# A Macaron block with a Mamba-2 mixer on one core: operations of the opening, the chunk steps and the units in another order

## The chip, the cores and the metric

The kernel runs on 1 core of one Trainium2 chip. The metric is the device time of one execution, in microseconds. Engines: PE is TensorE, DVE is VectorE, ACT is ScalarE, POOL is GpSimd, SP is SyncE, which issues most of the DMAs.

## What is computed

The input is x, 2048 tokens of 512 values. With LN a layer norm without weights:

```python
x = x + 0.5 * ffn(LN(x))      # ffn: a 512x512 weight of 4 bits with scales and zeros, plus LoRA, plus bias
x = x + attn(LN(x))
x = x + 0.5 * ffn(LN(x))      # the same ffn

def attn(u):
    h = u + mamba2(rmsnorm(u, ln1_w))        # h is the residual of what follows
    h2 = rmsnorm(h, ln2_w)
    return h + silu(h2 @ gate_w.T) * (h2 @ up_w.T) @ down_w.T      # 1792 wide

def mamba2(x):                               # 4 heads of 128, state 128, chunks of 128 tokens
    z, xBC, dt = split(x @ w_in.T)           # 512, 768 and 4 columns
    xBC = silu(causal_conv(xBC, 4 taps) + conv_b)
    ...                                      # per chunk: decay, (C B^T * decay) X, and the carried state
    return ((Y + D * xs) * silu(z)) @ w_out.T
```

## The kernel before

Everything is one program in which the order of each engine's instructions is written out by hand, with semaphores between the engines. An engine takes its instructions strictly in that order, so whatever waits holds up all that is written behind it. Products are made in f16 with each operand split into a high part (ACT rounds) and a low part (DVE subtracts, the functions `lo...`), three products for one (`PARTS`).

The 2048 tokens are 16 chunks of 128 (`c`), four to a tile of 512 (`i`, and `j` the place in the tile). The work has four stages.

**Opening** (to about 42 us; its end on DVE is L1749 to L1780, on ACT L1017 to L1051, on PE L2191 to L2219). The FFN weight is made from its 4 bits. The first six chunks are normed (`prep0`, `hi0`), transposed on PE (`first_t0`), copied (`tc0`), put through the FFN in f32 (`first_f`), added (`x1_stats`, which also makes the statistics for the next norm) and normed again (`hi1`, `lo1`). POOL makes each norm's factors from the statistics, in the order `ln1_chain(3)`, `ln0(5)`. Beside this, two scales are found, powers of two: one for the FFN weight, one for `w_in`. For each, a maximum per partition goes through a transpose on PE (`max_turn`), a reduction on DVE (`max_row`), a spread on PE (`max_spread`) and a chain of small DVE instructions (`max_all`, `power_of_two`). ACT waits for both (L1049) before it makes the high part of `w_in`.

**Prologue** (to about 87 us). `w_in` is cut, tile 0 is projected (`proj`), convolved (`taps`, three DVE instructions over 512 columns each), and put through silu. Chunks 6 to 9 come in. On SP's queue the transfers that transpose a chunk stand in order: `t1(6)` (second norm's input of chunk 6, after `lo1(6, 2)`), `next_x(6)`, `t0(8)` (first norm's output of chunk 8, after `lo0(8, 0)`), `t1(7)`, and so on. PE's `f(8)`, at the start of step 0, needs `t0(8)`. ACT's `hi1(7)` needs `t1(6)`.

**Steps** (`step(c)`, to about 345 us), one per chunk. PE does the FFN of chunk c + 8, the scan of chunk c, its output product `w(c)`, and some projections of the next tile; in the last four chunks gate/up products stand in their place. Three PSUM banks go round among these products, and a planner at L298 to L322 notes for each what must have freed its bank: for `f(11)` and `f(15)` it is `residual2` of chunk 2 and of chunk 6, and for the projection of plane 8 of tile 3 it is that of chunk 10. `residual2` (L1444) adds the product of `w(c)` to the norm and frees its bank; where `j` is 2, it stands behind the taps of plane 5 (`slot_a`). The scan of chunk c + 1 is prepared in step c: ACT's `scan_decay`, DVE's `scan1` (makes S), POOL's `scan_d` (masks S and adds the diagonal, L555), which PE's `s2_diag` (L2053) needs. Ahead of these stand, for chunk c - 1, the high part (`hi2`, ACT, needs POOL's factor `r2`) and the low part (`lo2`, DVE, L1379) of the norm whose transposed form gate/up reads. The gate on y (`gate_y`, L1428) frees PE for `w(c)`. From chunk 10 on POOL also makes sums of tokens for the last stage (`sums`).

**Units** (`unit(m)`, to about 702 us). Gate/up for the other six pairs of the 1792 columns run as seven products in place of eight (Strassen), four units to a pair, with the down products between them. In the last unit of a pair (`n == 3`), ACT (`st_a(p + 1, 0)`, L1074 and L1077) and DVE (`st_g(p + 1)`, L1533) make the two parts of the next pair's gate weight, with which PE's next unit starts. ACT's `evict` takes a down product out of PSUM, and POOL adds it to x by DMA. Then the last FFN runs over the chunks.

Of the kernel before, what the change touches and what calls it, by code (L numbers as in the profile page):

```python
# [6 lines left out]
ALU = mybir.AluOpType  # L7
# [7 lines left out]
P = 128  # L15
EPS = 1e-5
ACT_SCALE = 2.0 ** 9
# [10 lines left out]
def build(nc, x_in, w_in_t, conv_w, conv_b, a_log, d_skip, dt_bias, w_out_t, ln1_w, ln2_w,  # L28
# [23 lines left out]
    with ctx:  # L52
# [704 lines left out]
        def _(ac):  # L757
# [170 lines left out]
            def step(c):  # L928
                i, j = divmod(c, CH)
                a = c + 2 * CH  # L930
                if c > 0:
                    i_late, late = (c - 1) // CH + 1, SLOTS[(c - 1) % CH][1:]
                if c + 1 < NCH:
                    scan_ecs(c + 1, (c + 1) % CH)
                    scan1(c + 1, (c + 1) % CH)
                if c > 0 and i_late < NS:
                    for q in late[1:]:
                        slot_a(i_late, q)
                    slot_b(i_late, late[0])
                if a + 1 < NCH:  # L940
                    hi0(a + 1, (a + 1) % CH)
                if c > 0 and i_late < NS:
                    for q in late[1:]:
                        slot_b(i_late, q)
                if c > 0:
                    hi2(c - 1, (c - 1) % CH)
                if c + 1 < NCH:
                    scan_decay(c + 1, (c + 1) % CH)
                if j == 2 and i + 1 < NS:
                    slot_a(i + 1, SLOTS[j][0])  # L950
                if a < NCH:
                    hi1(a, a % CH)
                if c + 1 < NCH:
                    scan2(c + 1, (c + 1) % CH)
                if c == 3 * CH:
                    t_his(0, 0, 1, 2, 3)
                renorm(c)
                if c == 3 * CH + 2:
                    t_his(1, 0, 1, 2, 3)
                if i + 1 < NS:  # L960
                    if j != 2:
                        slot_a(i + 1, SLOTS[j][0])
                    slot_b(i + 1, SLOTS[j][0])
                    if j == 0:
                        sp_exp(i + 1)
                else:
                    gate_a(0, j)
                    gate_b(0, j)
                square(c, j)
                if i + 1 < NS:  # L970
                    slot_a(i + 1, SLOTS[j][1])
                if c in (2 * CH - 2, 2 * CH - 1):
                    fold(c - (2 * CH - 2))
                if c == 2 * CH + 2:
                    cut_a()
                if c == 2 * CH + 3:
                    cut_b()
# [60 lines left out]
            tc0(3)  # L1038
            hi1(0, 0)
            w_in_sum(2)  # L1040
            hi1(1, 1)
            hi0(4, 0)
            w_in_sum(3)
            tc0(4)
            hi1(2, 2)
            hi1(3, 3)
            hi0(5, 1)
            tc0(5)
            ac.wait_ge(e_scale, 2)  # L1049
            w_in_hi(W_IN_PIECES[0])  # L1050
            w_in_hi(W_IN_PIECES[1])  # L1051

# [140 lines left out]
            def weight_work(p, n, part):  # L1193
                if n == 0 and p > 1:
                    st_b(p, part)
                elif p + 1 < NP:
                    if n == 2:
                        norm(p + 1, part)
                    if n == 3:
                        st_a(p + 1, part)  # L1200

            def unit(m):
# [4 lines left out]
                copy_p1(m)  # L1207
                if m > 0:
                    hi_s(m - 1, 1)
                evict(ds[0])  # L1210
                tanh_s(m, 0)
                if m == 1:
# [42 lines left out]
        def _(ve):  # L1255
# [59 lines left out]
                ve.wait_ge(e_maxT, n + 1)  # L1315
                ve.tensor_reduce(mx1[:, n:n + 1], PS[0:1, B_MAX, MAX_AT[n]:MAX_AT[n] + P], AX_X, ALU.max).then_inc(e_max1, 1)

            def max_all(n):
                ve.wait_ge(e_all, n + 1)
                chain(ve.tensor_copy(mxa[:, n:n + 1], PS[:, B_MAX, MAX_AT[n] + P:MAX_AT[n] + P + 1]))  # L1320

            def ffn_scale():
                max_all(0)
                power_of_two(pw[:, 0:1], sw[:, 0:1], mxa[:, 0:1], chain)
                ve.sem_inc(e_scale, 1)
                chain(ve.tensor_scalar(d_f[:, :], pw[:, 0:1], 0.5 * 2.0 ** -W_TOP / ACT_SCALE, None, ALU.mult))

            def ffn_lo():
                for k in range(KB):
                    ve.wait_ge(e_fhi, k + 1)  # L1330
# [6 lines left out]
                chain(ve.tensor_tensor(mxk[:, :], mxk[:, :], ln1[:, :], ALU.mult))  # L1337
                ve.tensor_reduce(mx[:, 1:2], mxk[:, :], AX_X, ALU.max, apply_absolute_value=True).then_inc(e_max, 1)

            def w_in_scale():  # L1340
                max_all(1)
                power_of_two(pw[:, 1:2], sw[:, 1:2], mxa[:, 1:2], chain)
                chain(ve.tensor_scalar(lsw[:, :], ln1[:, :], sw[:, 1:2], None, ALU.mult))
                ve.sem_inc(e_scale, 1)

            def small_scales():
                chain(ve.tensor_scalar(d_i[:, :], pw[:, 1:2], 2.0 ** -W_TOP / ACT_SCALE, None, ALU.mult))
                chain(ve.tensor_scalar(d_ih[:, :], d_i[:, :], 0.5, None, ALU.mult))
                ve.wait_ge(s_small, 16 * 4)
# [274 lines left out]
            def prologue():  # L1624
# [18 lines left out]
                silu(0, 2)  # L1643
                taps(0, 4)
                silu(0, 3)
                prep0(8, 0)
                taps(0, 5)
                x1_stats(7, 3, PLAN["f", 7][0])
# [3 lines left out]
                silu(0, 5)  # L1652
                silu_z(0, 1)
                prep0(9, 1)
                lo1(6, 2)
                weights(0, 0)
                silu_z(0, 2)
                scan1(0, 0)
# [3 lines left out]
            def step(c):  # L1662
# [29 lines left out]
                    gate_y(c, j)  # L1692
                if c == 2 * CH + 2:
                    scale_read(0)
                if c > 0:
                    lo2(c - 1)
                advance(c, j)
                if c + 1 < NCH:
                    weights(c + 1, (c + 1) % CH)
                    scan1(c + 1, (c + 1) % CH)  # L1700
                if c == 3 * CH:
                    t_los(0, 0, 1, 2, 3)
                if c == 3 * CH + 2:
# [20 lines left out]
                    maximum_gu(1).then_inc(e_max, 1)  # L1724
                if c == 2 * CH + 3:
                    cut_a()
                if i + 1 < NS:
                    slot_a(i + 1, SLOTS[j][0], {1: 9}.get(j))
                    if j == 0:
                        softplus(i + 1, 0)  # L1730
                        softplus(i + 1, 1)
                        softplus(i + 1, 2)
                else:
                    gate_up(0, j)
                residual2(c, j)
                if c == 3 * CH:
                    cut_b()
                if i + 1 < NS:
# [24 lines left out]
            lo1(0, 0)  # L1763
            prep0(4, 0)
            x1_stats(2, 2, B_P[0])
            lo1(1, 1)
            ffn_scale()
            w_in_bound()
            max_row(1)
            x1_stats(3, 3, B_P[1])  # L1770
            prep0(5, 1)
            w_in_scale()
            lo1(2, 2)
            lo1(3, 3)
            w_in_lo(0)
# [56 lines left out]
            def unit(m):  # L1832
# [10 lines left out]
                    lo_s(m - 1, 1)  # L1843
                ve.wait_ge(e_gu, 2 * NS + base + 3)
                ve.tensor_tensor(u2, p1s, p_bank(m, IP6), ALU.add).then_inc(e_add, 1)
                if p + 1 < NP and n == 2 and m > 2:
                    scale_read(p + 1)
                    scales(p + 1)
                    descale(p + 1)
# [10 lines left out]
                if p + 1 < NP:  # L1860
                    if n == 1:
                        bound_g(p + 1, 0)
                        bound_g(p + 1, 1)
                        bounds(p + 1)
                    if n == 3:
                        st_g(p + 1)
                if m == NU - 1:
                    tail(1)
                ve.wait_ge(e_gu, 2 * NS + base + 5)
# [83 lines left out]
        def _(pe):  # L1953
# [254 lines left out]
            first_f(2)  # L2208
            max_spread(0)
            first_f(3)  # L2210
            first_t0(4)
            max_turn(1)
            max_spread(1)
            first_f(4)
            first_t0(5)
# [195 lines left out]
```

## Time and profile before

| | us |
|---|---|
| median of 3 runs | 783.96 |
| lowest, highest | 780.64, 784.36 |
| the profiled execution | 782.24 |
| its span, first to last instruction | 780.5 |
| busy: PE, DVE, ACT, POOL | 756.2, 628.9, 447.0, 336.4 |
| mean granted TensorE clock, share of full | 0.998 |

Busy time is that of the engine's instructions; waiting is not in it. A wait for several semaphores is put down to the one that came last by the profile.

### The profile page before, as it was taken

The numbers are of one execution on the slowest core, as the hardware profiler recorded it, in microseconds if no ns is written. First come the engines' busy times: TensorE is split into PE (matmuls) and PEld (weight loads), VectorE is DVE, ScalarE is ACT, GpSimd is POOL, SyncE is SP. The second block draws the span as 40 slices with busy tenths as digits, with TensorE's granted clock in tenths as the row PEclk, the third lists the DMA queues.
The fourth block names the chain that finished last, engine by engine and source line by source line (L and its number), as shares of the span: only waits on it lengthen the run. The fifth ranks groups of instructions, "written<-read, shape, count | busy, mean of one in ns | idle before, by whom it ended". The sixth has DMA issues, their size and how long they took to land.

```text
span 780.5 us, 10661 instructions
## 1 busy us (share of the span) xinstructions
PE 756.2 (97%) x3470; PEld 352.7 (45%) x3470; DVE 628.9 (81%) x1235; ACT 447.0 (57%) x881; POOL 336.4 (43%) x392
## 2 busy tenths in 40 slices
PE   8899899999999989899999999999999999999998
PEld 3344454454445444444443444444444444444443
DVE  7798678978967888777799979779779779667994
ACT  4777667767675766645435655555555455444441
POOL 5631344563543269664604224224234233224573
PEclk9999999999999999999999999999999999999999
DMA  8832543542431111520241544643643743443565
GB/s 299 188 74 54 130 101 81 109 107 46 83 64 28 38 31 28 135 41 15 43 119 28 136 89 73 149 81 68 157 78 64 162 82 57 81 79 72 119 161 135
DMA packets 95415, 71.86 MB, mean 92 GB/s; under 512 B 65233, under 2 KB 72401, under 8 KB 95361
## 3 DMA queue, kind: packets, MB, share of 16 engines
q0 software_dynamic: 17280, 31.46, 22.6%
q1 hardware_dynamic: 77600, 39.66, 19.7%
q8 instruction: 28, 0.46, 0.3%
q14 instruction: 27, 0.21, 0.1%
q10 hardware_dynamic: 480, 0.07, 0.1%
HBM read 20.32 MB, written 4.19 MB: 31 GB/s over the span
## 4 chain that ended last, share of the span: by engine, by line
PE 65%; DVE 19%; ACT 5%; issue 4%; POOL 4%; DMA 2%; SPq 0%; ACTq 0%; DVEq 0%; POOLq 0%
PE PS L1957 57%; PE PS L2080 3%; DVE raw L1453 2%; DVE st L1284 1%; DVE stage L1453 1%; PE PS L2088 1%; DVE state L1435 1%; DMA x_t<-hb 1%; DVE xs L1385 1%; PE PS L2062 1%; DVE S L1418 1%; PE PS L2053 1%; POOL r L521 1%; ACT pre L884 1%; PE PS L2070 1%
## 5 line engine op out<-in xcount | busy, mean ns | idle before, releaser
L712 POOL DMA_DIRECT2D xs<-x x59 | 50.9, 863 | 150.9 <-ACT x L1157 136.9
L1957 PE MATMUL PS<-h,w_in 128*128 128x512 f16 x480 | 108.7, 379 | 0.1
L1957 PE MATMUL PS<-h,x_t 128*128 128x512 f16 x408 | 94.0, 379 | 0.2 <-DVE pre L1795 0.2
L1957 PEld LDWEIGHTS PS<-h,w_in 128*128 128x128 f16 x480 | 46.8, 98 | 65.3 <-issue 15.4
L1957 PE MATMUL PS<-n_T,stage 128*128 128x512 f16 x288 | 71.5, 379 | 0.0
L1157 ACT ACTIVATE x<-PS,d_d 128x512 f32<-128x512 f32 x59 | 40.2, 682 | 39.4 <-PE PS L1957 39.4
L1957 PEld LDWEIGHTS PS<-h,x_t 128*128 128x128 f16 x408 | 39.5, 98 | 48.9 <-issue 2.7
L521 POOL TENSOR_TENSOR r<-mv,mhalf 128x1 f32<-128x1 f32 (+1 forms) x32 | 28.7, 897 | 75.9 <-DVE mv L1288 62.2
L712 POOL DMA_DIRECT2D xs<-n x29 | 25.2, 869 | 71.8 <-ACT n L1157 61.5
L1957 PE MATMUL PS<-pre,stage 128*128 128x512 f16 x192 | 49.3, 379 | 0.0
L1127 ACT ACTIVATE xds<-tm,dgh 128x512 f32<-128x512 f32 x24 | 17.3, 722 | 50.7 <-DVE tm L1886 50.7
L1957 PE MATMUL PS<-w_ffn,raw_gu 128*128 128x512 f16 x192 | 43.3, 379 | 1.2 <-DMA raw_gu<-raw_d 1.2
L1957 PEld LDWEIGHTS PS<-n_T,stage 128*128 128x128 f16 x288 | 28.1, 98 | 34.0 <-ACT x L1157 0.3
L1453 DVE SCALAR_TENSOR_TENSOR raw<-pre,cw,raw 128x512 f32<-128x512 f32 x36 | 28.0, 777 | 11.1 <-ACT raw L885 10.8
L1957 PE MATMUL PS<-w_ffn,n_T 128*128 128x512 f16 x120 | 29.2, 396 | 6.2 <-DVE x L1444 3.2
L1957 PE MATMUL PS<-raw,x_t 128*128 128x512 f16 x144 | 34.7, 379 | 0.4 <-DVE Ld L1841 0.4
L1957 PE MATMUL PS<-w_in,x_t 128*128 128x512 f16 x144 | 34.8, 379 | 0.0
L1957 PE MATMUL PS<-h,n 128*128 128x512 f16 x144 | 33.2, 379 | 1.5 <-DVE n L1533 1.5
L1157 ACT ACTIVATE n<-PS,d_d 128x512 f32<-128x512 f32 x29 | 19.8, 683 | 23.8 <-PE PS L1957 23.1
L2080 PE MATMUL PS<-w_out,raw 128*128 128x512 f32 x64 | 29.1, 597 | 1.0 <-DVE raw L1428 0.9
L1957 PEld LDWEIGHTS PS<-w_ffn,raw_gu 128*128 128x128 f16 x192 | 18.6, 98 | 24.1 <-DMA raw_gu<-raw_d 1.7
L2080 PE MATMUL PS<-w_out,stage 128*128 128x512 f32 x64 | 29.1, 598 | 0.1
(314 smaller groups left out, 1809.7 us busy)
## 6 DMA issues: line engine op xcount, KB each, us to landing
xs<-x POOLq DMA_DIRECT2D x75, 256.0 KB, 3.3
xs<-n POOLq DMA_DIRECT2D x29, 256.0 KB, 3.3
x_t<-x_in SPq DMA_DIRECT2D x16, 256.0 KB, 3.0
x_t<-hb POOLq DMA_DIRECT2D x16, 256.0 KB, 3.8
out<-x_t SPq DMA_DIRECT2D x16, 256.0 KB, 2.3
raw_gu<-gate_t SPq DMA_DIRECT2D x7, 512.0 KB, 4.5
raw_gu<-up_t SPq DMA_DIRECT2D x7, 512.0 KB, 6.5
raw_d<-down_t SPq DMA_DIRECT2D x7, 512.0 KB, 7.4
```

The source lines that it names most:

```text
L521: return po.tensor_tensor(dst, src, mhalf[:, 0:src.shape[-1]], ALU.pow)
L712: po.dma_start(chunk_of(xs, c), d_tmps[d % 3], accum_op=ALU.add).then_inc(s_acc[d % 3], 16)
L884: ac.activation(pre[:, w, NTAP - 1:], src, ACT.Copy)
L1127: ac.activation(th_s[ab], u4 if ab else c11, ACT.Tanh, scale=dgh[:, p % 2:p % 2 + 1]).then_inc(e_tanh_g, 1)
L1157: ac.activation(d_tmps[d % 3], bank(d_bank(d)), ACT.Copy, scale=d_d[:, p % 3:p % 3 + 1]).then_inc(e_ev, 1)
L1284: link(ve.bn_stats(stat, src), e_link, base + 1)
L1385: link(ve.scalar_tensor_tensor(chunk_of(xs, c), bank(b), 0.5 / ACT_SCALE if c < NF else d_f[:, :], x_t[:, j, :], ALU.mult, ALU.add), e_x1, ...
L1418: last = ve.scalar_tensor_tensor(S[:, s, h, :], heads(B_G)[:, h, :], dt[:, (c // CH) % 2, j * H + h:j * H + h + 1], Ld[:, h, :], ALU.mult, ...
L1435: last = ve.scalar_tensor_tensor(state[:, h, :], state[:, h, :], ecs[:, s, h, P - 1:P], heads(B_SS)[:, h, :], ALU.mult, ALU.add)
L1453: ins = ve.scalar_tensor_tensor(xbc[i % 2][:, b, :], pre[:, w, k:k + ST], cw[:, b, k:k + 1], xbc[i % 2][:, b, :], ALU.mult, ALU.add)
L1957: ins = pe.matmul(out_, lhs(a, b, k), rhs(a, b, k), start=first and n == 0, stop=last and n == len(todo) - 1)
L2080: last = pe.matmul(bank(b), y[:, h, (c % CH) * P:(c % CH + 1) * P], w_out[:, h, :], start=h == 0, stop=h == H - 1)
```

## The change

It touches four places. In the opening, the two scales are found in one chain of instructions (`both_scales`), the sum of the fourth block of `w_in` and the bound move forward, and some norms change places; ACT's wait is for one event instead of two, and `d_f` is made in `small_scales`. In the prologue, `lo1(6, 2)` stands before `prep0(8, 0)`. In the steps, `residual2` stands before `slot_a` where `j == 2` and there is a next tile (chunks 2, 6, 10), and for chunks above 12 `hi2` and `lo2` stand behind `scan_decay` and `scan1`. In the last unit of each pair, the two parts of the gate weight are made earlier.

```diff
@@ scalar, step(c)
-                if c > 0:
+                if 0 < c <= 3 * CH:
                     hi2(c - 1, (c - 1) % CH)
                 if c + 1 < NCH:
                     scan_decay(c + 1, (c + 1) % CH)
+                if c > 3 * CH:
+                    hi2(c - 1, (c - 1) % CH)
@@ scalar, opening
             w_in_sum(2)
+            w_in_sum(3)
             hi1(1, 1)
             hi0(4, 0)
-            w_in_sum(3)
             tc0(4)
             hi1(2, 2)
+            hi0(5, 1)
             hi1(3, 3)
-            hi0(5, 1)
             tc0(5)
-            ac.wait_ge(e_scale, 2)
+            ac.wait_ge(e_scale, 1)
@@ scalar, weight_work
-                    if n == 3:
+                    if n == 3 and part > 0:
                         st_a(p + 1, part)
@@ scalar, unit(m)
                     hi_s(m - 1, 1)
+                if p + 1 < NP and n == 3:
+                    st_a(p + 1, 0)
                 evict(ds[0])
                 tanh_s(m, 0)
@@ vector
-            def max_all(n):
-                ve.wait_ge(e_all, n + 1)
-                chain(ve.tensor_copy(mxa[:, n:n + 1], PS[:, B_MAX, MAX_AT[n] + P:MAX_AT[n] + P + 1]))
-
-            def ffn_scale():
-                max_all(0)
-                power_of_two(pw[:, 0:1], sw[:, 0:1], mxa[:, 0:1], chain)
-                ve.sem_inc(e_scale, 1)
-                chain(ve.tensor_scalar(d_f[:, :], pw[:, 0:1], 0.5 * 2.0 ** -W_TOP / ACT_SCALE, None, ALU.mult))
...
-            def w_in_scale():
-                max_all(1)
-                power_of_two(pw[:, 1:2], sw[:, 1:2], mxa[:, 1:2], chain)
+            def both_scales():
+                ve.wait_ge(e_all, 2)
+                chain(ve.tensor_copy(mxa[:, :], PS[:, B_MAX, :].rearrange("p (n q) -> p n q", q=MAX_AT[1])[:, :, P]))
+                power_of_two(pw[:, :], sw[:, :], mxa[:, :], chain)
                 chain(ve.tensor_scalar(lsw[:, :], ln1[:, :], sw[:, 1:2], None, ALU.mult))
                 ve.sem_inc(e_scale, 1)
 
             def small_scales():
+                chain(ve.tensor_scalar(d_f[:, :], pw[:, 0:1], 0.5 * 2.0 ** -W_TOP / ACT_SCALE, None, ALU.mult))
@@ vector, prologue
                 silu(0, 3)
+                lo1(6, 2)
                 prep0(8, 0)
...
                 prep0(9, 1)
-                lo1(6, 2)
                 weights(0, 0)
@@ vector, step(c)
-                if c > 0:
+                if 0 < c <= 3 * CH:
                     lo2(c - 1)
                 advance(c, j)
                 if c + 1 < NCH:
                     weights(c + 1, (c + 1) % CH)
                     scan1(c + 1, (c + 1) % CH)
+                if c > 3 * CH:
+                    lo2(c - 1)
...
+                if j == 2 and i + 1 < NS:
+                    residual2(c, j)
                 if i + 1 < NS:
                     slot_a(i + 1, SLOTS[j][0], {1: 9}.get(j))
...
-                residual2(c, j)
+                if j != 2 or i + 1 == NS:
+                    residual2(c, j)
@@ vector, opening
             x1_stats(2, 2, B_P[0])
+            w_in_bound()
             lo1(1, 1)
-            ffn_scale()
-            w_in_bound()
+            prep0(5, 1)
             max_row(1)
             x1_stats(3, 3, B_P[1])
-            prep0(5, 1)
-            w_in_scale()
+            both_scales()
@@ vector, unit(m)
                 ve.tensor_tensor(u2, p1s, p_bank(m, IP6), ALU.add).then_inc(e_add, 1)
+                if p + 1 < NP and n == 3:
+                    st_g(p + 1)
...
-                    if n == 3:
-                        st_g(p + 1)
@@ tensor, opening
             first_f(3)
+            max_turn(1)
             first_t0(4)
-            max_turn(1)
             max_spread(1)
```

## Rows read from the trace of the kernel before

**Rows 1.** The page's part 1: busy time and its share of the span.

```profile
PE 756.2 (97%) x3470; PEld 352.7 (45%) x3470; DVE 628.9 (81%) x1235; ACT 447.0 (57%) x881; POOL 336.4 (43%) x392
```

**Rows 2.** Who PE waited for, whole span: total us, times, longest.

```profile
PE PS L1957 <- DVE x L1444: 3.2, 2, 1.7
PE PS L2053 <- POOL S L555: 3.1, 3, 1.2
PE PS L1957 <- DMA n_T<-n_p: 3.0, 2, 2.7
...
PE PS L1957 <- DVE n L1533: 1.5, 1, 1.5
...
PE PS L2080 <- DVE raw L1428: 0.9, 1, 0.9
...
PE PS L1957 <- DVE pre L1795: 0.2, 1, 0.2
```

**Rows 3.** Timeline of the opening, DVE then PE: start, us, instruction, idle before.

```profile
29.03 0.15 DVE L1320 COPY mxa<-PS 128x1 f32<-128x1 f32 x1
...
31.19 0.67 DVE L1385 SCALAR_TENSOR_TENSOR xs<-PS,x_t 128x512 f32<-128x512 f32 x1
...
32.97 0.68 DVE L1284 BATCH_NORM_STATS2 st<-x_t 128x6 f32<-128x512 f32 x1
...
42.11 5.34 PE L1957 MATMUL PS<-h,w_in 128*128 128x512 f16 x24
```

**Rows 4.** Timeline of the prologue's end; the last row is busy time by window.

```profile
83.44 0.68 DVE L1367 TENSOR_TENSOR hn_p<-hn,hn_p 128x512 f16<-128x512 f32 x1
...
84.32 2.75 PE L1957 MATMUL PS<-h,w_in 128*128 128x512 f16 x12
...
86.10 2.26 SPq L443 DMA_TRANSPOSE n_T<-n_p  x1
...
87.37 1.26 POOL L555 TENSOR_TENSOR S<-S,d_diag 128x512 f32<-128x512 f32 x1
...
90.24 4.45 PE L1957 MATMUL PS<-w_ffn,n_T 128*128 128x512 f16 x12 [2.71 <-DMA n_T<-n_p]
...
91.00:92.00 1.00, 1.00 (x4) 0.30 (x2) 0.07 (x1) 1.00 (x4) 0.00 (x0) 0.50 0.00 0
```

**Rows 5.** Timeline of steps 2 and 3, then of step 7: DVE and PE.

```profile
143.38 2.31 DVE L1453 SCALAR_TENSOR_TENSOR raw<-pre,cw,raw 128x512 f32<-128x512 f32 x3
145.60 0.68 DVE L1444 TENSOR_TENSOR x<-n,PS 128x512 f32<-128x512 f32 x1
...
152.15 0.74 DVE L1428 SCALAR_TENSOR_TENSOR stage<-PS,d_ih,stage 128x512 f32<-128x512 f32 x1
...
155.08 3.60 PE L2080 MATMUL PS<-w_out,stage 128*128 128x512 f32 x8
...
222.45 0.74 DVE L1428 SCALAR_TENSOR_TENSOR raw<-PS,d_ih,raw 128x512 f32<-128x512 f32 x1
...
224.50 3.60 PE L2080 MATMUL PS<-w_out,raw 128*128 128x512 f32 x8
```

**Rows 6.** Timeline of PE in steps 10 to 12.

```profile
280.94 1.12 PE L2045 MATMUL PS<-raw 128*128 128x512 f32 x2 [0.45 <-DVE raw L1461]
...
291.98 1.12 PE L2053 MATMUL PS<-S,tm 128*128 128x512 f32 x2 [0.85 <-POOL S L555]
```

**Rows 7.** Timeline of step 13, ACT and DVE.

```profile
311.56 0.72 ACT L794 ACTIVATE h2n_p<-x,r 128x512 f16<-128x512 f32 x1 [2.70 <-POOL r L521]
...
312.31 1.95 DVE L1379 SCALAR_TENSOR_TENSOR h2n_p<-x,r,h2n_p 128x512 f16<-128x512 f32 x1
```

**Rows 8.** All of one line, L1379: shortest, median, longest in ns.

```profile
L1379 DVE SCALAR_TENSOR_TENSOR h2n_p<-x,r,h2n_p x16: 740/754/1945, 119.7 to 348.2; 128x512 f16<-128x512 f32 x16
```

**Rows 9.** Timeline of unit 3, ACT then DVE.

```profile
424.11 0.61 ACT L1074 ACTIVATE n<-raw_gu 128x512 f16<-128x512 f32 x1
...
425.72 0.68 DVE L1533 TENSOR_TENSOR n<-raw_gu,n 128x512 f16<-128x512 f32 x1
```

## The prediction

> **What bounds the kernel now.** I read the page first. TensorE (PE) is busy 756.2 of 780.5 us [rows 1], so only 24 us of the span is not matrix work, and an edit that moves work on another engine pays only where it takes away one of PE's waits. The next view is therefore who PE waited for [rows 2]. The first five pairs shown come to 11.7 us. Then I read the timeline round each wait: what the releasing instruction stood behind, and what comes next if it is released sooner. The profiled execution took 782.2 us, 1.7 outside the span. The median of the runs is 784.0 with one run at 780.6, so a measurement can tell about 0.5% (4 us) from no change.
>
> **Opening scales: 0.5 us.** In the old order VectorE (DVE) makes the FFN scale in a chain of small instructions from 29.03, bounds w_in, waits for the transposed maximum, and only at 31.19 starts `x1_stats(3)` [rows 3]: 2.2 us for little work. Now the FFN copy and its four steps go, `d_f` moves into `small_scales` (its cover is w_in's low part, which PE needs only two projections later), and in their place stands `prep0(5,1)`, 1.0 us (from 32.97, 0.68 and two small ones) [rows 3]. `w_in_sum(3)` goes ahead of `hi1(1,1)` on ScalarE (ACT), so `lo1(1,1)` starts perhaps 0.4 later. I get `x1_stats(3)` at 29.03 + 0.4 + 1.0 + 0.2 for `max_row` = 30.65, 0.5 sooner. GpSimd (POOL) makes chunk 3's and then chunk 5's norm factors behind it, so `hi0(5,1)` can start near 34.6; but now `hi1(3,3)` (two activations, 1.4) stands behind it and before `tc0(5)`. The last transpose copy, hence `first_f(5)` and the projection that started at 42.11 [rows 3], gain the same 0.5. Also for PE, `max_turn(1)` ahead of `first_t0(4)` saves nothing more: the transpose waits for ACT there anyway. What is late next is `t1(3)`: `lo1(3,3)` is about 1 us later, and its transfer must land before 41.6. Bounds: 1.5 gained at best (`both_scales` comes 1.0 + 0.5 sooner on DVE), 1.4 lost at worst (the pair now ahead of `tc0(5)`). I take 0.5, since POOL's factors limit both.
>
> **The seventh chunk's split: 4.4 us, the largest term.** `lo1(6,2)` ran at 83.44 though its input was ready at about 73. SP's queue is in order: `t1(6)` waits for it, and `next_x(6)` and `t0(8)` stand behind. So chunk 8's transpose was issued at 86.10, and PE stood 2.71 us before `f(8)` [rows 4]. Worse, the granted clock is 0.50 from 91 to 92, that is 1.2 GHz instead of 2.4: it fell behind this idle time, and the 12 matmuls of `f(8)` took 4.45 us where the 12 at 84.32 took 2.75 [rows 4]. Moved ahead of `prep0(8,0)`, the split is done by 75, and `t0(8)` waits for `lo0(8,0)` alone, which by the timeline ended near 80.5 and is 0.6 later as the moved instruction is now ahead of it. It is issued at 81.1, and even 4.1 us later (86.10 to 90.24) it is there by 85.3, before PE is ready at 87.5. Gain: 2.71 + (4.45 - 2.75) = 4.4. Next comes `s2_diag(0)`, which needs POOL's sum at 87.37 + 1.26 [rows 4]; 0.6 later that is 89.2, and PE gets there at 90.1. That cover is 0.9 us; if it goes, the term loses what is missing. `hi1(7,3)` no longer waits for `t1(6)` either, so chunk 7's transpose, due at the next projection, goes forward with it. Bounds: 2.7 (only the wait goes) and 4.4.
> The page "TensorE: Matmul & The Clock Gate" of the Trainium skill (Part 1) says that the array goes back to half clock when it has been idle, and comes up again only with work. By it the two halves stand or fall together: if any wait of this size stayed, the 1.7 us would stay too. The trace agrees so far, as it shows both here and neither where the wait was 1.7.
>
> **Residual ahead of the taps: +1.6, +0.7, -0.6.** In chunks 2 and 6, `f(11)` and `f(15)` use the bank that `residual2` empties, and it stood behind three conv taps: 143.38 to 145.60, 0.68 long itself [rows 5]. PE waited 3.2 us in the two [rows 2]. First in line it frees the bank 2.2 sooner, so both waits go. The price is 0.6 on the taps, the tanh, the silu and all of DVE's next step, up to `gate_y`. After chunk 2 `gate_y` ended at 152.89 for an output product at 155.08; PE comes 1.7 earlier and y 0.6 later, so 1.6 of 1.7 is kept. After chunk 6 it ended at 223.19 for 224.50: 1.3 of slack less 0.6 leaves 0.7 of 1.5 [rows 5]. In chunk 10 PE did not wait for the residual; it waited 0.45 for the silu at 280.94 [rows 6], and that is now 0.6 later, as is ACT's square, from which POOL's chain leads to the wait of 0.85 at 291.98 [rows 6]. Both give 0.6 lost, once. Bounds for all three: +3.2 (the waits) and -1.8 (0.6 each time).
>
> **Last block's second norm: 3.3 us.** In the step of chunk 13 ACT stood 2.70 us for POOL's factor before `hi2(12)`, with the decay of chunk 14 behind it; on DVE `lo2(12)` took 1.95, with the state and `scan1(14)` behind it [rows 7]. S then went to POOL, and PE waited for POOL's sum. Decay and scan don't need the norm. With them first, ACT can start the decay near 308.8, DVE does `scan1(14)` about 1.9 sooner (the whole `lo2`), and the sum is ready near 316.6 where PE wants it at 317.3. The same holds a step on. The three waits for this sum came to 3.1, of which 0.85 is the one above that stays: 2.2 goes. The 0.9 for y in the last step [rows 2] goes as well, since tanh, gates and tile sums all come sooner: 3.1, and the wait for the gated product (0.2) [rows 2] too: 3.3. The norm itself is later by the decay and scan, some 1.5 us; its cover is that only the transposes for gate/up read it, steps away. Bounds: 0 and 3.3.
> `lo2` takes 0.75 in the median, yet 1.95 here [rows 7, 8], with POOL busy beside it. The Trainium skill's page "SBUF — State Buffer" says ("SBUF: two separate sides") that a VectorE operation with two SBUF inputs and a GpSimd operation exclude each other for a whole instruction. This speaks against the move: `lo2` now starts as POOL begins on S. By it POOL's sum would come one `lo2` later, 317.3, level with PE's need, and the term would be 3.2 rather than 3.3.
>
> **Units: 1.1 us.** PE waited 1.5 for the low part of the next gate weights, done at 426.4 [rows 2, 9]. ACT's high part moves ahead of an eviction and a tanh, and DVE can make the low part, at 425.72 before, ahead of one product and one addition of 0.6 each [rows 9]: 1.2 sooner, and 0.1 goes to the next weights, which DVE finishes no sooner. In the four later pairs PE did not wait, so nothing there; the eviction is 0.9 us later (the pair from 424.11), covered by PE's next product, and so is POOL's transfer behind it. Bounds: 0 and 1.5.
>
> **Sum.** 0.5 + 4.4 + 1.6 + 0.7 - 0.6 + 3.3 + 1.1 = 11.0 us. Against the profiled run: 782.2 - 11.0 = 771.2; against the median 773.0. I say 772, between them.
>
> **Rivals.**
> - *The steps keep nothing.* DVE is on much of the chain through the steps, and a wait taken from PE comes back one link later: tap delay three times, the POOL sum held up by `lo2`. Then only opening, split and units count: 784.0 - 6.0 = 778.0. For: DVE and ACT wait for one another there. Against: the slack read off above. Chance 0.2.
> - *The split's wait stays.* `t0(8)` lands no sooner than f(8) needs it, or the POOL sum behind it takes the place and the clock falls all the same: 784.0 - 6.6 = 777.4. Against: 2 us of room. Chance 0.1.
> - *Nothing comes of it*, because the queue order that I read is not what holds the waits, within 4 us of 784: chance 0.09.
> - *Slower.* `t1(3)` lands late: its split is behind `hi1(3,3)`, itself behind `hi0(5,1)`, and the first projection stands long enough for the clock to fall. A matmul at half clock costs (4.45 - 2.75)/12 = 0.14 us more. To lose the 11.0 and 4 more, some 105 matmuls must run so, more than the 72 that come before the first conv product, with the idle time on top; time 789. Against: `f(8)` shows the clock back within 12. Chance 0.03.
> - The forecast: 0.58.
>
> **Range and chances.** The forecast's own terms give 768 (every wait goes, no delay counted, the faster base) to 776; the first two rivals end near 778, and I stop at 779. Faster by over 0.5%: 0.58 + 0.2 + 0.1 = 0.88; within: 0.09; slower: 0.03.
>
> **What would show it.** PE's waits should lack the DMA wait before `f(8)`, both waits for `residual2`, and two of three for POOL's sum; the granted clock should stay at 1.00 past 80 us; `f(8)` should take 2.75. The projection should start near 41.6. The silu wait near 270 (280.94 less what is gained) should be 1.0, not 0.45. I am wrong if PE's idle time falls by less than 6 us, or if a new wait of over 1 us stands at the output product of chunk 3 or 7, or at `s2_diag`.

## The result and the profile after

The changed kernel takes 774.97 us (median of 5 runs, 774.16 to 776.01), the kernel before 783.19 in the same series: ratio 0.9899, 95% interval 0.9877 to 0.992, faster by 1.0%. The forecast was 772.0 with a range of 768 to 779. The sign and the largest term held; some 3 us of the expected 11 are missing. The profiled execution took 775.83 us, 1.7 outside its span of 774.1, against 782.24 and 780.5. Two of the five executions of the changed kernel, this one and the one at 776.01, had a mean granted clock of 0.998; the other three, 774.16 to 774.97, had 1.000. Of the executions further down two took far longer, one of the kernel with the residual of chunk 10 moved back (988.02 us) and one of the kernel before (1614.6): they count in the medians and not in the ratios.

Part 1 of the page of the changed kernel, against [rows 1]:

```profile
PE 755.7 (98%) x3470; PEld 352.5 (46%) x3470; DVE 628.5 (81%) x1230; ACT 446.0 (58%) x881; POOL 337.5 (44%) x392
```

The work of PE is the same to 0.5 us, so the change could act through waits and the clock alone. PE's idle time fell from 24.33 to 18.35 us, by 5.98: the prediction had named less than 6 as a sign of being wrong, and this is just under it. Who PE waited for in the changed kernel (total us, times, longest), against [rows 2]:

```profile
PE PS L1957 <- ACT n L1159: 1.6, 3, 0.6
...
PE PS L1957 <- ACT x L1159: 1.2, 2, 0.6
...
PE PS L2045 <- DVE raw L1457: 1.0, 1, 1.0
PE PS L2080 <- DVE raw L1424: 0.9, 1, 0.9
PE PS L2053 <- POOL S L555: 0.8, 1, 0.8
...
PE PS L1957 <- DVE n L1529: 0.3, 1, 0.3
PE PS L1957 <- DMA n_T<-n_p: 0.2, 1, 0.2
PE PS L2080 <- DVE stage L1424: 0.2, 1, 0.2
```

All that was to go has gone: the residual's 3.2, two of the three waits for POOL's sum, the transpose's 2.7, 1.2 of the gate weights' 1.5. But two rows are new: five waits, 2.8 us together, for the eviction (now L1159) in the units. No new wait of over 1 us stands at the places that the prediction had named (0.86 at the output product of chunk 7, 0.83 at `s2_diag`). The timeline of PE in the changed kernel, at the places that the forecast named:

```profile
37.48 5.40 PE L2180 MATMUL PS<-h,n_T 128*128 128x512 f32 x8 [1.23 <-ACT n_T L774]
...
88.39 2.75 PE L1957 MATMUL PS<-w_ffn,n_T 128*128 128x512 f16 x12
90.98 1.02 PE L2053 MATMUL PS<-S,tm 128*128 128x512 f32 x2
...
150.00 1.55 PE L2080 MATMUL PS<-w_out,stage 128*128 128x512 f32 x3 [0.18 <-DVE stage L1424]
...
218.86 1.13 PE L2080 MATMUL PS<-w_out,raw 128*128 128x512 f32 x2 [0.86 <-DVE raw L1424]
...
276.00 1.12 PE L2045 MATMUL PS<-raw 128*128 128x512 f32 x2 [1.05 <-DVE raw L1457]
...
416.31 2.76 PE L1957 MATMUL PS<-h,n 128*128 128x512 f16 x12 [0.33 <-DVE n L1529]
424.80 0.82 PE L1957 MATMUL PS<-pre,w_out 128*128 128x512 f16 x3 [0.43 <-ACT n L1159]
...
468.93 0.82 PE L1957 MATMUL PS<-pre,w_out 128*128 128x512 f16 x3 [0.57 <-ACT n L1159]
```

To see where the 6.4 us of the two spans lie, I cut both executions at the first projection and at seven one-matmul landmarks, the transposes of the maxima (PE, L2121). The first, second, third, fourth and seventh of them in the changed kernel:

```profile
255.07 0.27 PE L2121 MATMUL PS<-ident,mx 128*3 128x128 f32 x1 [0.52 <-ACT raw L885]
335.78 0.27 PE L2121 MATMUL PS<-ident,mx 128*3 128x128 f32 x1
392.70 0.27 PE L2121 MATMUL PS<-ident,mx 128*3 128x128 f32 x1 [0.55 <-DVE mx L1481]
444.32 0.27 PE L2121 MATMUL PS<-ident,mx 128*3 128x128 f32 x1
...
619.15 0.27 PE L2121 MATMUL PS<-ident,mx 128*3 128x128 f32 x1
```

and in the kernel before:

```profile
260.61 0.27 PE L2121 MATMUL PS<-ident,mx 128*3 128x128 f32 x1 [0.52 <-ACT raw L885]
344.72 0.27 PE L2121 MATMUL PS<-ident,mx 128*3 128x128 f32 x1
401.64 0.27 PE L2121 MATMUL PS<-ident,mx 128*3 128x128 f32 x1 [0.55 <-DVE mx L1485]
453.66 0.27 PE L2121 MATMUL PS<-ident,mx 128*3 128x128 f32 x1
```

(its seventh is at 626.18). With the projection at 42.11 before and 43.14 after, the stretches are:

| stretch | before | after | difference |
|---|---|---|---|
| to the first projection (opening) | 42.11 | 43.14 | +1.03 |
| to the 1st transpose (split, residual of chunks 2 and 6) | 218.50 | 211.93 | -6.57 |
| to the 2nd (last block: residual of chunk 10, second norm) | 84.11 | 80.71 | -3.40 |
| to the 3rd | 56.92 | 56.92 | 0 |
| to the 4th (units, first pair end) | 52.02 | 51.62 | -0.40 |
| to the 7th (units, three pair ends) | 172.52 | 174.83 | +2.31 |
| to the end (one more pair end) | 154.32 | 154.95 | +0.63 |

The losses are at both ends: 1.0 us in the opening, 2.9 in the units.

### The profile page after: what moved, and what is told of

The parts are those of the page before. It is cut to its first block, busy times and chain, and to the rows that moved or that the text cites. A ratio compares the mean times of both kernels' runs of the same rounds, so it can differ in the third digit from the quotient of the medians.

```text
span 774.1 us, 10655 instructions
## 1 busy us (share of the span) xinstructions
PE 755.7 (98%) x3470; PEld 352.5 (46%) x3470; DVE 628.5 (81%) x1230; ACT 446.0 (58%) x881; POOL 337.5 (44%) x392
## 4 chain that ended last, share of the span: by engine, by line
PE 67%; DVE 20%; ACT 5%; issue 4%; DMA 2%; POOL 2%; ACTq 0%; POOLq 0%; DVEq 0%
PE PS L1957 55%; PE PS L2080 4%; DVE raw L1449 2%; DVE S L1817 2%; DVE xds L1819 1%; PE PS L2088 1%; DVE st L1288 1%; PE PS L2180 1%; DVE stage L1449 1%; PE PS L2053 1%; DMA x_t<-hb 1%; PE PS L2062 1%; DVE state L1431 1%; PE PS L2070 1%; PE PS L2045 1%
## 5 line engine op out<-in xcount | busy, mean ns | idle before, releaser
L1159 ACT ACTIVATE x<-PS,d_d 128x512 f32<-128x512 f32 x59 | 40.2, 682 | 41.2 <-PE PS L1957 41.2
L1159 ACT ACTIVATE n<-PS,d_d 128x512 f32<-128x512 f32 x29 | 19.8, 684 | 24.8 <-PE PS L1957 24.8
L1957 PEld LDWEIGHTS PS<-pre,stage 128*128 128x128 f16 x192 | 18.7, 98 | 23.5 <-ACT x L1159 1.1
```

What stands on the lines that cost most here:

```text
L1159: ac.activation(d_tmps[d % 3], bank(d_bank(d)), ACT.Copy, scale=d_d[:, p % 3:p % 3 + 1]).then_inc(e_ev, 1)
L1957: ins = pe.matmul(out_, lhs(a, b, k), rhs(a, b, k), start=first and n == 0, stop=last and n == len(todo) - 1)
```

## The experiments

The landmarks resolve 0.1 us where a median of four runs does not resolve 1, so the sizes below are read from the stretches, the verdicts on kernels from the medians. Each kernel is the changed one with one edit, unless said. "Before" stood at a median of 782.57, 783.29 and 783.12 us in the three series, and the ratios are to it. Where an experiment is set beside the changed kernel, the two medians are from different series.

**The split back in its old place, and the split alone.**

```
                 silu(0, 3)
-                lo1(6, 2)
 ...
                 prep0(9, 1)
+                lo1(6, 2)
```

> The changed kernel with the seventh chunk's split back in its old place, all else changed. Theory: it is the largest term and stands alone: 4.4 us in the forecast, 4.57 between the two profiles; the wait of 2.7 us for the chunk's transpose before the FFN product at 90 us returns, with the clock at half for the product's 4.45 us. From the projection to the second product at 91 us it takes 4.4 to 4.6 us more than in the changed kernel. Rival (part of it was given by the residual's or the opening's new place, or is given back later): under 3 us on the median.

Measured: 778.68 us (ratio 0.9947, 0.9929 to 0.9965), 3.7 above the changed kernel. The stretch to the first transpose is 258.13 - 41.55 = 216.58, against 211.93 in the changed kernel and 212.1 in most of the other kernels here that have both edits: 4.5 us. The timeline of PE with the split in its old place, and its windows (us busy by engine, then the granted clock):

```profile
89.75 4.45 PE L1957 MATMUL PS<-w_ffn,n_T 128*128 128x512 f16 x12 [2.63 <-DMA n_T<-n_p]
```

```profile
91.00:92.00 1.00, 1.00 (x4) 0.31 (x3) 0.40 (x1) 1.00 (x3) 0.00 (x0) 0.50 0.23 54
```

Both halves return, the wait of 2.63 and the product at half clock, as in [rows 4].

The other way round, the kernel before with this one edit:

> The kernel before with the seventh chunk's split in its new place and nothing else. Theory: the split's term is independent of the other edits: no wait for the chunk's transpose at 90 us, and from the first projection to the first transpose of maxima 4.4 us less than the 218.50 of the kernel before, 214.1; median 4 us under that of before, a little less than 4.4 since some runs of the kernel before show a clock of 1.000 and can win only the wait of 2.7. Rival (the split needs the residual's or the opening's new places to be of use): 216 or more, and a median within 2.5 us of before.

Measured: 779.24 us (0.995, 0.993 to 0.997), 3.9 under before; 257.51 - 43.54 = 213.97 us to the first transpose, 4.5 less. The term does not depend on the rest. By difference (218.50 - 216.58) the residual's move in chunks 2 and 6 is worth 1.9, where the forecast had 2.3; the two places in the timeline gave 1.5 and 0.6.

**The opening as it was.** Both scale chains, the order on ACT and PE and the places of `w_in_sum(3)`, `prep0(5, 1)` and `hi0(5, 1)` as before.

```
-            hi0(5, 1)
             hi1(3, 3)
+            hi0(5, 1)
             tc0(5)
-            ac.wait_ge(e_scale, 1)
+            ac.wait_ge(e_scale, 2)
 ...
-            both_scales()
+            w_in_scale()
```

> The changed kernel with its opening as before (both scale chains, the old order of ACT and PE). Theory: the opening's new order costs 1.03 us up to the first projection (it starts at 43.14 instead of 42.11), because two idle stretches close together (0.79 and 1.23 us) let the clock fall and the first FFN product of chunk 5 took 5.40 us instead of 3.70. Then this kernel's projection starts at 42.1 and its span is about 1.0 us shorter than the changed kernel's 774.1, the granted clock between 20 and 40 us level with before. Rival (the 1.0 us is lost in the transfers, w_in's low part or the split behind the opening, or what is lost at the start is covered later): span within 0.4 us of 774.1.

Measured: 776.55 us (0.992, 0.9894 to 0.9947), span 775.6: 1.5 us longer than the changed kernel's, where 1.0 shorter was expected. The theory fell. Timeline of PE with the old opening:

```profile
37.09 0.66 PE L2179 MATMUL PS<-ident,n 128*128 128x128 f32 x4 [1.21 <-ACT n L767]
38.44 5.40 PE L2189 MATMUL PS<-h,n_T 128*128 128x512 f32 x8 [0.69 <-ACT n_T L774]
...
44.10 2.11 PE L1966 MATMUL PS<-h,w_in 128*128 128x512 f16 x9
```

The two waits are the 1.2 and 0.7 of the kernel before, whose product took 3.70; here it took 5.40. So the old opening loses the clock too, in some executions. And the new one keeps it in most. The next rows are PE's in the kernel with the units' edit in the first pair alone (below), whose opening is the changed kernel's, with the same two waits:

```profile
35.71 0.66 PE L2172 MATMUL PS<-ident,n 128*128 128x128 f32 x4 [0.80 <-ACT n L767]
37.60 3.70 PE L2182 MATMUL PS<-h,n_T 128*128 128x512 f32 x8 [1.23 <-ACT n_T L774]
...
41.57 4.70 PE L1959 MATMUL PS<-h,w_in 128*128 128x512 f16 x21
```

Windows of the changed kernel, then of that one, 36 to 41 us: PE is busy 3.77 us in both, the granted clock (third figure from the end) 0.70 and 1.00.

```profile
36.00:41.00 5.00, 3.77 (x8) 1.61 (x7) 2.70 (x6) 5.00 (x11) 3.31 (x5) 0.70 0.77 151
```

```profile
36.00:41.00 5.00, 3.77 (x12) 1.66 (x11) 2.58 (x6) 5.00 (x11) 3.44 (x5) 1.00 0.80 158
```

Of nine profiles with the new opening, the changed kernel's alone shows the fall; of three with the old, two (this one and the kernel with the split alone). Like with like, the projection starts at 42.11 (old) against a median of 41.6 (new, eight profiles, 41.28 to 43.16) where the clock held, and at 43.5 and 44.1 against 43.14 where it fell. That has the sign and about the size of the forecast's 0.5 us, but the scatter of the opening from run to run (1.9 us among the eight) is larger, so the size is not shown.

**The transpose copy ahead of chunk 3's pair.**

```
             hi0(5, 1)
-            hi1(3, 3)
             tc0(5)
+            hi1(3, 3)
```

> The changed kernel with the transpose copy of chunk 5 right behind its normalization, ahead of the pair of activations for the transpose of chunk 3. Theory: PE's second idle stretch (1.23 us before the FFN product of chunk 5) shrinks to 0.5 us or less, the clock does not fall, the product takes 3.7 us or less and starts at about 36.8; the projection then starts between 41.0 and 41.6, 1.5 to 2 us sooner than in the changed kernel, span 772.1 to 772.6. Rival 1 (the clock falls with the first of the two stretches all the same): the product starts at 36.8 but takes 5.4, projection at 42.4. Rival 2 (the transpose of chunk 3 comes late for the projection, since its split is now later): a wait for a transfer of up to 1 us at the first projection.

Measured: 775.13 us (0.9908, 0.9883 to 0.9934); the projection starts at 42.35. PE's timeline:

```profile
37.03 3.70 PE L2180 MATMUL PS<-h,n_T 128*128 128x512 f32 x8 [0.69 <-ACT n_T L774]
40.79 0.38 PE L2163 MATMUL PS<-junk 128*128 128x512 bf16 x1
42.35 1.46 PE L1957 MATMUL PS<-h,w_in 128*128 128x512 f16 x6 [1.19 <-DMA h<-hn_p]
```

The second rival held: the FFN product is early (37.03) and at full clock, and the projection waits 1.19 us for chunk 3's transpose, issued at 39.27 by SP's queue and used 3.1 us later. In the changed kernel it is issued at 37.76, so it is there at about 40.9, 0.7 ahead of an undisturbed projection. The order of the change has little left in either direction.

**Idle matmuls where PE waits.** They compute nothing that is used.

```
             first_f(4)
+            keep_warm(3)
             first_t0(5)
+            keep_warm(4)
```

> The changed kernel with seven idle matmuls into a free bank: three before the transpose of chunk 5's input, four behind it, where PE waited 0.79 and 1.23 us. They do no work for the result. Theory: what the opening loses is the clock, not the waits, so with PE kept busy the FFN product of chunk 5 takes 2.9 to 3.7 us instead of 5.40 and the projection starts 1.2 to 1.7 us sooner, near 41.7, though nothing else is earlier. Rival (the product took long for another reason, such as the wait for its operand or weight loads): the product still takes over 5 us and the projection starts at 43.1 or later, as seven matmuls were added.

Measured: 774.94 us (0.9905, 0.988 to 0.993); the product takes 3.70, the projection starts at 42.05. The number came out as forecast, but it shows less than I meant it to: the product takes 3.70 without ballast as well in most profiles, and then the projection starts at 41.6, sooner than with it. That the 5.40 came from the clock is read from the granted clock of 0.70 above, not from this experiment.

**The residual of chunk 10 back behind the taps.**

```
-                if j == 2 and i + 1 < NS:
+                if j == 2 and i < 2:
                     residual2(c, j)
 ...
-                if j != 2 or i + 1 == NS:
+                if j != 2 or i >= 2:
                     residual2(c, j)
```

> The changed kernel with the residual of chunk 10 back behind the conv taps, those of chunks 2 and 6 still ahead of them. Theory: PE did not wait for that residual, so its early place only delays the taps and the silu; the wait for the silu at 276 us falls from 1.05 to 0.45 and the stretch between the first two transposes of maxima is 0.6 us shorter than 80.71, span and median 0.6 lower. Rival (the delay is absorbed, as POOL's sum is what PE waits for next, and that comes at the same time): less than 0.2 us.

Measured: 773.8 us (0.9873, 0.9836 to 0.991), 1.2 below the changed kernel; the stretch is 333.57 - 253.42 = 80.15, against 80.71: 0.56. The forecast's -0.6 was right, and nothing absorbs it in this stage. The wait for the silu is back to 0.4. (The other 0.6 us of the 1.2 is not explained by the edit; medians of series differ by that much.)

**The last block's second norm: both halves back, one at a time.** On ACT (with `hi2`) and on DVE (with `lo2`):

```
-                if 0 < c <= 3 * CH:
+                if c > 0:
                     lo2(c - 1)
 ...
-                if c > 3 * CH:
-                    lo2(c - 1)
```

> The changed kernel with the second norm of the last block ahead of the decay again, on ACT and on DVE. Theory: the stretch from the first to the second transpose of maxima (255.07 to 335.78 in the changed kernel, 80.71 us; 84.11 before) is back at 84.1 plus the 0.6 of the residual of chunk 10, so 84.1 to 84.7: the term is 3.4 to 4.0 us, against 3.3 in the forecast. PE's waits for POOL's sum return to 3 us. Rival (the DVE and POOL operations that now run beside one another slow each other, so that part comes from elsewhere): under 2.5 us.

Measured: 778.47 us (0.9939, 0.992 to 0.9958), 3.5 above; the stretch is 338.94 - 254.23 = 84.71, so the term is 4.0. PE's waits in the whole of that kernel:

```profile
PE PS L2049 <- POOL S L555: 3.0, 3, 1.2
PE PS L2076 <- DVE raw L1422: 1.7, 2, 0.9
```

The three waits for POOL's sum are back, and beside the 0.86 of chunk 7 that the residual's move left, the 0.88 of the last y.

Only DVE's half back:

> The changed kernel with the low part of the last block's second norm ahead of the decay on DVE again, its high part still behind it on ACT. Theory: DVE then waits for a high part that ACT makes only behind the decay, so both halves are lost and a little more: the stretch between the first two transposes of maxima is 84.7 to 85.7 us, against 80.7 with both halves and 84.7 with none. Rival (it is ACT's half that counts and DVE's small instruction is covered): under 83.

Measured: 339.92 - 255.21 = 84.71 (one run, 779.83 us). Only ACT's half back:

> The changed kernel with the high part of the last block's second norm ahead of the decay on ACT again, its low part behind it on DVE. Theory: ACT stands for POOL's factor with the decay behind it (2.7 us), but DVE no longer puts its 1.9 us in between, so about half of the term stays: 82 to 83.3 us between the first two transposes of maxima. Rival (DVE's half does nothing without ACT's): 84.7.

Measured: 336.45 - 253.71 = 82.74 (one run, 776.36 us). So moving ACT's half alone is worth nothing (the low part then stands on DVE, waiting for it, with the scan behind), moving DVE's alone 2.0, both 4.0. Each rests on one execution.

**The eviction in the units.** First, the early high and low part in the first pair alone:

```
-                if p + 1 < NP and n == 3:
+                if m == 3:
                     st_a(p + 1, 0)
                 evict(ds[0])
```

(`st_g` on DVE likewise, and both in their old places for later pairs.)

> The changed kernel with the early high and low part of the next gate weights only in the first pair of units; in the five later pair ends the order is as before. Theory: the two activations (0.83 us) ahead of the eviction make PE wait 0.43 to 0.60 us for the evicted bank, at each pair end, and cost about 0.77 each with what follows; in the first pair the gain of 1.2 outweighs it. So the four later ones give back 3.1 us: span 771.0, and PE's waits for the eviction fall from 2.8 us to about 0.4. Rival (the landmarks drift in the units because of something else, such as the DVE order or the clock): the drift stays, span 774.

Measured: 771.59 us (0.9863, 0.9834 to 0.9892), span 769.6. From the first to the seventh landmark it takes 615.46 - 253.71 = 361.75, against 364.08: 2.3 less, and 0.8 less behind it (154.14 against 154.95). Second, in all pairs, but the eviction first:

```
+                evict(ds[0])
                 if p + 1 < NP and n == 3:
                     st_a(p + 1, 0)
-                evict(ds[0])
```

> The changed kernel with the eviction ahead of the two activations of the next gate weights in every pair of units, both still ahead of the tanh. It tells whether PE's loss in the units comes from the eviction's place (the two activations stand before it) or from the tanh's and the gate weights'. Theory: the eviction alone. Then the wait for the evicted bank goes in all five pairs, also in the first, and from the first transpose of maxima (255 us in the changed kernel) to the last (619) it takes 3.5 us less than the changed kernel's 364.1, about 360.6, or 0.4 less than the experiment with the first pair alone (361.8 there). Rival (the tanh behind the activations is what comes late, or the early low part on DVE): 364, as the eviction's place does not matter.

Measured: 771.28 us (0.9842, 0.9811 to 0.9873), 361.72 from first to seventh. ACT and PE at the second pair end, in the changed kernel:

```profile
467.38 0.61 ACT L1076 ACTIVATE n<-raw_gu 128x512 f16<-128x512 f32 x1
467.90 0.40 ACT L1079 ACTIVATE d_diag<-raw_gu 128x256 f16<-128x256 f32 x1
468.21 0.67 ACT L1159 ACTIVATE n<-PS,d_d 128x512 f32<-128x512 f32 x1
```

with PE at 468.93 [0.57], and with the eviction first:

```profile
465.64 0.67 ACT L1159 ACTIVATE n<-PS,d_d 128x512 f32<-128x512 f32 x1
466.21 0.62 ACT L1076 ACTIVATE n<-raw_gu 128x512 f16<-128x512 f32 x1
466.73 0.40 ACT L1079 ACTIVATE d_diag<-raw_gu 128x256 f16<-128x256 f32 x1
467.04 0.71 ACT L1129 ACTIVATE xds<-Ld,dgh 128x512 f32<-128x512 f32 x1
```

The tanh is as late as in the changed kernel, counted from the first of these instructions (1.4 us in both), the low part as early, and the loss is gone: the eviction's place alone made it. The 360.6 was missed by 1.1: in the first pair the order makes no difference. There PE's wait of 0.43 for an eviction at the next unit (424.80) stays in both, since ACT comes to it straight from the high parts, which wait for DVE.

**The two corrections together** (eviction first, residual of chunk 10 behind the taps):

> The changed kernel with the eviction ahead of the activations of the next gate weights, and with the residual of chunk 10 behind the conv taps. Theory: the two corrections lie in different stages and add up: 771.28 less 0.6 is 770.7 us, the stretch between the first two transposes of maxima 80.15 and that from the second to the last 280.97, span 768.7. Rival (in the last block the gain of the residual is eaten by the wait for maxima or for the low part of the gate weights): 771.3.

Measured: 771.35 us (0.9859, 0.984 to 0.9878), not distinguishable from the 771.28 with the eviction alone. The stretches are 80.15 and 281.25: half of the residual's 0.6 is given back in the units (281.25 against 280.97). Both kernels beat the changed one, by 3.6 and 3.7 us; the second correction adds nothing that the medians show.

## Why the prediction came out as it did

- **Split, 4.4: right.** 4.5 by undoing it and 4.5 by doing it alone. What was said of the clock held: wait and half clock left together and came back together. It is not a fixed price: of the 16 runs of before in one series, two had a mean granted clock of 1.000 and took 780.9 and 781.0, against a median of 783.3, so there presumably only the wait is to be won (their traces were not taken).
- **POOL's sum next, cover 0.9: mis-sized, without effect.** It was ready at 90.66 for a PE at 90.98: 0.3 was left.
- **Residual, +1.6 and +0.7: right**, 1.5 and 0.6 in the timeline, 1.9 by the stretch. The wait for y came to 0.18 and 0.86, as the slack read off in [rows 5] said. **-0.6: right**, 0.56.
- **Last block's second norm, 3.3: right in mechanism, too small.** The four waits that it named (1.21 and 1.00 for POOL's sum, 0.23, 0.88) came to 3.3 and all went; the term measured 4.0. The other 0.7 is what a wait costs beside its own row. The product behind one is longer, 1.12 or 1.13 for 1.02 at `s2_diag`, 3.70 for 3.60 at the output product: 0.31. And a row counts from the end of PE's row before, while an undisturbed product starts 0.16 before that end (at 304.62, when the row before, 0.39 from 304.39, ends at 304.78): 0.64 for the four. Against it 0.28 is left in the changed kernel at 312.37, where no wait is shown but the product starts 0.17 later than an undisturbed one and takes 1.13. 3.32 + 0.31 + 0.64 - 0.28 = 3.99, for a measured 4.0. The cover of 0.7 that it computed was used up: the sum ended at 312.32 for a PE that took it at 312.37. Of what used it up, 0.45 is POOL's L553, which stands ahead of the sum and took 1.09 us beside `lo2` at 309.88, against 0.64 at 316.48 in the kernel before. The prediction's other reading, "level with PE's need", is what came.
- **Units, 1.1: the step that failed.** "In the four later pairs PE did not wait, so nothing there; the eviction is 0.9 us later (the pair from 424.11), covered by PE's next product". The first half is true and says nothing, since a row without a wait does not tell how much slack it has. The cover was some 0.1 us. In the kernel before, the eviction of the second pair end ended at 477.35 for the product that needs its bank at 477.50, and 0.05 lies between the two where PE waits (468.88 and 468.93):

```profile
476.68 0.67 ACT L1157 ACTIVATE n<-PS,d_d 128x512 f32<-128x512 f32 x1
...
477.50 0.81 PE L1957 MATMUL PS<-pre,w_out 128*128 128x512 f16 x3
```

Counted from the landmark before it, the eviction starts 0.87 later in the changed kernel (23.89 against 23.02) and the product 0.77 (24.61 against 23.84), of which PE's row shows 0.57. The row is short for the reason given above. A period between landmarks grows by the same 0.77, from 57.51 to 58.28. Four of them lose 3.1. In the first pair the gate product did start 1.2 sooner, but 0.8 of it was lost again by the fourth landmark, 0.43 as the wait at 424.80. Together -2.5 instead of +1.1.
- **Opening, 0.5: not contradicted, its size not shown.** In the profiled execution a clock that fell there by chance hides it (+1.03 in the ledger: 1.7 lost to the clock, 0.7 gained before it). The link that was computed is there, `x1_stats(3)` starts at 30.67 for a forecast of 30.65. What reaches the projection lies within the scatter of 1.9.

For the medians that makes 0.5 (the forecast's own, as no run gives a better figure) + 4.5 + 1.9 - 0.6 + 4.0 - 2.5 = 7.8 us, and 8.2 were measured. None of the rivals came. The range held because it reached down to partial gains, not because this loss had been seen.

## What to carry to other kernels

An instruction moved ahead of another on an in-order queue taxes every iteration, also those in which nothing was late. Before a cover is claimed, measure it: the time from the delayed instruction's end to the start of what waits for it (0.15 us here, against a delay of 0.87), not the absence of a wait. Put the early work behind the one that frees a PSUM bank: it costs the early work 0.6 us here and saves 0.77 in each later pair. And where two halves of a value sit on two engines, moving one half alone may bring nothing (here 0 and 2.0 against 4.0 for both).

## What was not expected of the hardware

- **The same two short waits do and don't cost the clock.** With 0.7 to 0.8 and then 1.23 us of waiting (new order) PE's granted clock over 36 to 41 us was 0.70 in one profile and 1.00 in eight; with 1.2 and 0.7 (old) it fell in two of three. A fall costs 1.7 us, 5.40 for the product instead of 3.70. The Trainium skill's page "TensorE: Matmul & The Clock Gate" (Part 1) says that the point of the transition varies from run to run, as it doesn't hang on where the kernel starts. It says so of the rise at the start of work; in these profiles the same holds of a fall behind short waits in mid-kernel. One pair of profiles can therefore not price such an opening, and my first theory was built on one.
- **DVE's `lo2` and POOL's instructions take turns.** In the last block's new order `lo2` took 2.52 us at 319.50 where the median is 0.75, and of POOL's instructions beside it the sum took 1.61 where the median is 1.27:

```profile
319.50 2.52 DVE L1375 SCALAR_TENSOR_TENSOR h2n_p<-x,r,h2n_p 128x512 f16<-128x512 f32 x1 [0.65 <-ACT h2n_p L794]
```

```profile
319.36 1.52 POOL L549 TENSOR_TENSOR raw<-raw,ecs 128x512 f32<-128x512 f32 x1
320.58 0.89 POOL L553 TENSOR_SCALAR_AFFINE_SELECT S<-S 128x512 f32<-128x512 f32 x1
321.55 1.61 POOL L555 TENSOR_TENSOR S<-S,d_diag 128x512 f32<-128x512 f32 x1
```

It cost nothing, since S was there at 323.16 for a PE at 324.55. POOL's L549 had begun 0.14 before `lo2`, and `lo2` ended at 322.02, 0.55 after the end of L553 (321.47). The 1.95 of [rows 7] is alike: it ended at 314.26, 0.56 after this one of the kernel before (313.70):

```profile
312.18 1.52 POOL L549 TENSOR_TENSOR raw<-raw,ecs 128x512 f32<-128x512 f32 x1
```

In the two traces 16 of the 32 `lo2` began while POOL had such an instruction (128x512) running, and each of the 16 ended 0.54 to 0.56 us after the end of that one (in the case above after that of L553, which began before L549 ended), whether it took 0.75 or 2.52. The Trainium skill's page "SBUF — State Buffer" ("SBUF: two separate sides") has the two exclude each other for a whole instruction. The rows fit this: `lo2` waits for the end of what POOL began first, and here for L553 as well; and POOL's sum, begun while `lo2` had 0.47 left, is 0.34 longer. What `lo2` loses is therefore what POOL has left to do, and not a fixed price.
